# Expert layer's begin: last answers and logits ahead of the shared expert's products, its activations multiplied on GpSimd, running counts in three additions

## The reference, cut to what matters

```
normed = layernorm(x) * ln_gamma + ln_beta          # 1024 rows
logits = normed @ router_w.T                        # 8 experts
probs  = softmax(logits);  top_v, top_i = top_k(probs, 2);  gates = softmax(top_v)
for e in range(8): out += comb[:, e, None] * swiglu(normed, gate_up_w[e], down_w[e])
out += swiglu(normed, shared_gate_up_w, shared_down_w)     # silu(gate) * up @ down
x = x + out
```

## Time and profile before

| | before |
|---|---|
| median of 3 runs | 1829.05 us (1829.04 to 1835.1) |
| profiled execution, its own time | 1831.19 us |
| its span | 1829.30 us |
| granted TensorE clock, mean | 0.997 |
| TensorE busy | 1768.9 us, 97% |
| VectorE, ScalarE, GpSimd busy | 1347.6, 1018.4, 938.8 us |

### The profile page before, as it was taken

One profiled execution on the slowest core, in us unless ns is written; L12 is line 12 of the kernel. 1 busy time (PEld: TensorE's weight loads), 2 busy tenths in 40 slices (PEclk: granted clock), 3 DMA queues, 4 the chain that ended last, 5 costly groups with the idle time before them and its releaser, 6 DMA issues.

```text
span 1829.3 us, 44764 instructions
## 1 busy us (share of the span) xinstructions
PE 1768.9 (97%) x17870; PEld 1542.8 (84%) x17870; DVE 1347.6 (74%) x2790; ACT 1018.4 (56%) x2138; POOL 938.8 (51%) x1178
## 2 busy tenths in 40 slices
PE   7999999999999999999999999999999999999998
PEld 5888888888888778899999999999999986668887
DVE  6888888888888877667766767676777655767775
ACT  5677676767677745455444445444445434536664
POOL 3787877777777517445433334333433303524553
PEclk9999999999999999999999999999999999999999
DMA  6121111121110110044222222222223007051111
GB/s 166 38 74 39 38 39 38 53 59 38 38 38 3 60 51 1 26 120 117 64 64 64 64 64 64 64 64 64 77 76 87 15 1 304 1 187 32 33 32 16
DMA packets 50750, 113.11 MB, mean 62 GB/s; under 512 B 4928, under 2 KB 37264, under 8 KB 49008
## 3 DMA queue, kind: packets, MB, share of 16 engines
q1 hardware_dynamic: 46128, 105.13, 19.4%
q0 software_dynamic: 4416, 5.12, 1.6%
HBM read 105.78 MB, written 5.37 MB: 61 GB/s over the span
## 4 chain that ended last, share of the span: by engine, by line
PE 77%; DVE 13%; ACT 4%; issue 3%; DMA 2%; POOL 1%; SPq 0%; DVEq 0%; POOLq 0%; ACTq 0%
PE ps L104 8%; PE ps L166 7%; PE ps L1782 5%; PE ps L514 5%; PE ps L495 5%; PE ps L472 4%; DVE arenaR L1899 3%; PE ps L2769 3%; DVE arena L1905 3%; PE ps L1783 3%; PE ps L489 3%; PE ps L424 2%; PE ps L1706 2%; PE ps L2743 2%; PE ps L2744 2%
## 5 line engine op out<-in xcount | busy, mean ns | idle before, releaser
L617 DVE TENSOR_REDUCE arena<-ps 128x1 f32<-128x400 f32 (+1 forms) x512 | 257.7, 565 | 84.8 <-PE ps L472 84.4
L777 ACT ACTIVATE arena<-ps 128x384 f32<-128x384 f32 (+1 forms) x512 | 223.3, 524 | 95.0 <-PE ps L495 93.8
L1782 PE MATMUL ps<-arenaR 128*128 128x386 f32 x768 | 266.3, 392 | 1.4 <-DVE arenaR L1899 1.4
L878 POOL TENSOR_TENSOR arena<-arena 128x512 f32<-128x512 f32 (+1 forms) x152 | 197.2, 1298 | 77.6 <-ACT arena L777 69.3
L2009 ACT CAST arenaR<-ps 128x512 fp32r<-128x512 f32 (+1 forms) x256 | 123.0, 507 | 184.0 <-PE ps L166 175.0
L1783 PE MATMUL ps<-arenaR 128*128 128x194 f32 x768 | 194.8, 254 | 0.0
L166 PE MATMUL ps<-ident,wsb 128*128 128x128 f32 (+1 forms) x832 | 160.0, 273 | 5.0 <-DVE arenaR L1899 3.0
L2034 ACT ACTIVATE wsb<-ps,arena 128x1200 f32<-128x1200 f32 x64 | 80.9, 1264 | 132.0 <-DVE arena L1958 132.0
L1782 PEld LDWEIGHTS ps<-arenaR 128*128 128x128 f32 x768 | 145.5, 189 | 1.7 <-DVE arenaR L1899 1.6
L1783 PEld LDWEIGHTS ps<-arenaR 128*128 128x128 f32 x768 | 146.8, 191 | 0.0
L1899 DVE TENSOR_TENSOR arenaR<-ps,arenaR 128x512 fp32r<-128x512 f32 (+1 forms) x256 | 138.2, 581 | 4.0 <-ACT arenaR L2009 3.7
(11 more groups left out here) (387 smaller groups left out, 5098.2 us busy)
## 6 DMA issues: line engine op xcount, KB each, us to landing
wsb<-in_ctx SPq DMA_DIRECT2D x16, 1152.0 KB
wsb<-in_ctxT SPq DMA_DIRECT2D x16, 800.5 KB, 5.1
wsb<-in_ctxT SPq DMA_DIRECT2D x32, 400.2 KB, 7.6
gu<-in_m_gu SPq DMA_DIRECT2D x8, 1536.0 KB, 19.5
arena<-in_ctxT SPq DMA_DIRECT2D x15, 800.5 KB, 5.0
arena<-in_ctxT SPq DMA_DIRECT2D x30, 400.2 KB, 7.3
dn<-in_m_dn SPq DMA_DIRECT2D x8, 768.0 KB, 11.3
wsb<-in_f_w SPq DMA_DIRECT2D x2, 1024.0 KB, 5.8
```

The source lines that it names most:

```text
L617: e.tensor_reduce(mx4[n % 2][:, u, i:i + 1], ps[:, at("look", n, i, u), 0:400 + (i == 3)], AX.X, ALU.max).then_inc(c.maxed.at((n, i, u)), 1)
L777: e.activation(v[:, u, 0:128 * GN[s]], ps[:, at("st", n, s, u), 0:128 * GN[s]], ACT.Exp).then_inc(c.exp_a.at((x0, n, s, u)), 1)
L878: e.tensor_tensor(sums_p[0:k], sums_p[0:k], v[0:k, :, 128 * t:128 * t + 128], ALU.add).then_inc(added_p.at((n, s)), 1)
L1782: e.matmul(o, PTh[:, t, :], v[:, t, 0:386], start=(t == 0), stop=False)
```

## The change

On TensorE the last answers are turned ahead of any logits, and all logits come before the first shared product: tile 7 is turned behind the logits of tile 4, its halves into two banks (2 and 3), each with its own signal. VectorE adds the last answers before it norms tile 6. The second half of tile 7's `hT` is taken by ScalarE, behind the load of its Exp table, the first by VectorE as before. `shared_gu(0, 0)` is made whole behind the logits; ranks come between it and `shared_gu(0, 1)`; `shared_gu(1, 1)` stands behind the table, and `shared_down(1)` behind `turn_block(0)` (on VectorE behind `take_block(0)`).

The product Silu x up moves from VectorE to GpSimd. As GpSimd can't read PSUM, ScalarE copies up into `sT` ahead of the Silu, and GpSimd multiplies in place: the first two ahead of the gates' product, (1, 0) ahead of the first gather, (1, 1) between the second and the third.

The running counts, before a masked 128x512 product and a sum over it (and one addition for `cnt`), are made by copying the counts behind 64 zeros (which GpSimd writes) and three additions, each of the counts and the counts 1, 2 and 4 tiles back; `base` and `cnt` are views of the result.

```diff
@@ moe, pe: logits, and the order
-            w.wait_ge(*(c.hT_act((into, t)) if t < LT else c.hT_dve((into, t))))
+            w.wait_ge(*c.hT_act((into, t)))
+            if t == LT:
+                w.wait_ge(*c.hT_dve((into, t)))
...
         tail.turn_rows(e, w, LT - 2, 6, 256)
-        logits(0)
-        logits(1)
         tail.turn_answers(e, w, LT, 2, 0)
+        for t in range(3):
+            logits(t)
         w.wait_ge(*c.hT_act((into, LT - 2)))
         tail.turn_rows(e, w, LT - 1, 6, 0)
-        for t in range(2, 5):
+        for t in range(3, 5):
+            logits(t)
+        w.wait_ge(*c.x_new((tt, LT)))
+        w.wait_ge(*c.normed((into, LT)))
+        for k in range(2):
+            c.turn(e, ps[:, 2 + k, 256:384], c.h[:, LT, 128 * k:128 * k + 128]).then_inc(c.hT_turned.at((into, LT, k)), 1)
+        for t in range(5, NT):
             logits(t)
         ended(w)
-        shared_gu(0, 0, (0,))
-        w.wait_ge(*c.x_new((tt, LT)))
-        tail.turn_rows(e, w, LT, 2, 256)
-        for t in range(5, NT):
-            logits(t)
-        shared_gu(0, 0, (1,))
-        shared_gu(0, 1)
+        shared_gu(0, 0)
         w.wait_ge(*routing("chosen"))
         e.matmul(ps[:, 7, 0:64], tri, flat(M), start=True, stop=True)
         e.matmul(ps[:, 7, 64:128], ones, flat(M), start=True, stop=True).then_inc(routed.at("ranks"), 1)
+        shared_gu(0, 1)
         shared_gu(1, 0)
         shared_down(0, range(2))
-        shared_gu(1, 1)
         w.wait_ge(*routing("placed"))
         for k in range(2):
             table(k)
+        shared_gu(1, 1)
         shared_down(0, range(2, 4))
-        shared_down(1)
...
         turn_block(0)
+        shared_down(1)
@@ moe, dve
-        def shared_act(half, f):
-            w.wait_ge(*sh_silu((half, f)))
-            if half:
-                w.wait_ge(*h_out("h"))
-            e.tensor_tensor(sT[half][:, f, :], ps[:, sh_bank(half, f) + 1, :], sgs[f], ALU.mult).then_inc(sh_act.at((half, f)), 1)
...
-        norm_tile(c, e, w, into, LT - 1)
         tail.add_answers(e, w, LT, 2, 0)
         w.wait_ge(*c.x_new((tt, LT)))
         moments(c, e, w, into, LT)
+        norm_tile(c, e, w, into, LT - 1)
...
-        w.wait_ge(*c.hT_turned((into, LT)))
-        for k in range(2):
-            e.tensor_scalar(hT[:, k, 128 * LT:1024], ps[:, 2, 256 + 128 * k:384 + 128 * k], c.lng[:, k:k + 1], c.lnb[:, k:k + 1],
-                            ALU.mult, ALU.add).then_inc(c.hT_dve.at((into, LT) if k else None), 1)
+        w.wait_ge(*c.hT_turned((into, LT, 0)))
+        e.tensor_scalar(hT[:, 0, 128 * LT:1024], ps[:, 2, 256:384], c.lng[:, 0:1], c.lnb[:, 0:1],
+                        ALU.mult, ALU.add).then_inc(c.hT_dve.at((into, LT)), 1)
...
-        e.tensor_tensor(c4, ps[:, 7, 64:128].rearrange("p (u e) -> p e u", e=8).unsqueeze(1).broadcast_to([128, 8, 8, 8]),
-                        lt.unsqueeze(2).broadcast_to([128, 8, 8, 8]), ALU.mult).then_inc(c.dv.at(), 1)
+        w.wait_ge(*c.po("past the last"))
+        e.tensor_copy(Z[0][:, 8:16, :], T).then_inc(c.dv.at(), 1)
         w.wait_ge(*c.dv.now())
-        e.tensor_reduce(base, c4, AX.X, ALU.add).then_inc(c.dv.at(), 1)
-        w.wait_ge(*c.dv.now())
-        e.tensor_tensor(cnt, base[:, 7, :], T[:, 7, :], ALU.add).then_inc(c.dv.at(), 1)
-        w.wait_ge(*c.dv.now())
+        for i, back in enumerate((1, 2, 4)):
+            src, dst = Z[i % 2], Z[1 - i % 2]
+            e.tensor_tensor(dst[:, 8:16, :], src[:, 8:16, :], src[:, 8 - back:16 - back, :], ALU.add).then_inc(c.dv.at(), 1)
+            w.wait_ge(*c.dv.now())
...
-        for f in range(2):
-            shared_act(0, f)
...
-        for f in range(2):
-            shared_act(1, f)
...
         shared_down(0)
+        take_block(0)
         shared_down(1)
-        take_block(0)
@@ moe, act
+            if half:
+                w.wait_ge(*h_out("h"))
+            e.copy(sT[half][:, f, :], ps[:, sh_bank(half, f) + 1, :]).then_inc(sh_silu.at(), 1)
             e.activation(sgs[f], ps[:, sh_bank(half, f), :], ACT.Silu).then_inc(sh_silu.at((half, f)), 1)
...
         e.activation(c.sd[:, 1:2], c.ident[:, 0:1], ACT.Exp).then_inc(c.ac.at(), 1)
+        w.wait_ge(*c.hT_turned((into, LT, 1)))
+        e.activation(hT[:, 1, 128 * LT:1024], ps[:, 3, 256:384], ACT.Identity, bias=c.lnb[:, 1:2], scale=c.lng[:, 1:2]
+                     ).then_inc(c.hT_act.at((into, LT)), 1)
@@ moe, pool
+        def shared_act(half, f):
+            w.wait_ge(*sh_silu((half, f)))
+            e.tensor_tensor(sT[half][:, f, :], sT[half][:, f, :], sgs[f], ALU.mult).then_inc(sh_act.at((half, f)), 1)
...
+        for i in range(2):
+            e.memset(cmp_[:, 128 * i:128 * i + 64], 0.0).then_inc(c.po.at(), 1)
         e.memset(C_[:, :, NS:NS + 1], 0.0).then_inc(c.po.at("past the last"), 1)
+        for f in range(2):
+            shared_act(0, f)
         w.wait_ge(*routing("placed"))
...
-        for i in range(3):
-            gather(i)
+        shared_act(1, 0)
+        gather(0)
+        gather(1)
+        shared_act(1, 1)
+        gather(2)
```

More of the change, by code:

```diff
@@ L2626, in moe @@
     yS = [ar(128, 256) for _ in range(2)]
-    lg, pr, oh1, oh2, tmp, M, base, slot = [ar(128, NT, 8) for _ in range(8)]
-    cnt, nt, start, end = [ar(128, 8) for _ in range(4)]
+    lg, pr, oh1, oh2, tmp, M, slot = [ar(128, NT, 8) for _ in range(7)]
+    nt, start, end = [ar(128, 8) for _ in range(3)]
     pos, blk, row, g12 = [ar(128, 16) for _ in range(4)]
@@ L2910, in dve @@
         T = ps[:, 7, 64:128].rearrange("p (t e) -> p t e", e=8)
-        c4 = cmp_.rearrange("p (t e u) -> p t e u", e=8, u=8)
-        c3 = cmp_[:, 0:64].rearrange("p (a b) -> p a b", b=8)
+        Z = [cmp_[:, 128 * i:128 * i + 128].rearrange("p (t e) -> p t e", e=8) for i in range(2)]
+        base, cnt = Z[1][:, 7:15, :], Z[1][:, 15, :]
+        c3 = cmp_[:, 256:320].rearrange("p (a b) -> p a b", b=8)
         w.wait_ge(*prob("gate"))
@@ L2945, in dve @@
             w.wait_ge(*c.dv.now())
-        w.wait_ge(*c.po("past the last"))
         ce = cmp_[:, 0:16 * NS].rearrange("p (i s) -> p i s", s=NS)
```

## The result

The changed kernel is slower: ratio to the kernel before 1.0031, with a 95% interval of 1.0021 to 1.0042, which is 5.7 us (3.9 to 7.7). Its eleven runs took 1836.05 to 1844.96 us (median 1838.85), eleven runs of the kernel before, the three shown ahead of the prediction among them, 1829.04 to 1841.71 (median 1834.10). The forecast was 0.4 us faster, within 1826.5 to 1831.3. The profiled execution of the changed kernel took 1836.66 us, its span is 1834.8, 5.5 more than before.

What follows compares the result with a forecast made beforehand. TensorE, busy 97% of the span, bounds the kernel, so the change acts only by moving the start of `gate_up(0, 0)`. Terms on its path summed to -0.4 us: from the median 1829.05 to 1828.7, range 1826.5 to 1831.3.

Steps and rivals of the forecast that it cites:

- A rule against the change: VectorE's routing chain beside GpSimd's products: lengthening taken from the median row, 691 against 619, 0.1 us per us, hidden.
- The price at the worst: GpSimd's two products hold VectorE's chain fully, 2.6 us: rows ready at 1632.3, 1.1 behind TensorE; sum +0.7.
- The case: Rival, VectorE's routing chain held by GpSimd: 1.1 us later than forecast, time 1829.8; chance 0.05.
- the clock behind the table: TensorE behind the table's narrow products: no lower clock, as wide products stand ahead and behind; -1.2 to -1.6 us, 1.3 taken.
- the rival's price of +1.3: Rival, second slow stretch stays: lower clock behind the table falls on `shared_gu(1, 1)`, +1.3 us, time 1830.0; chance 0.25.
- The rivals: Second slow stretch stays (0.25), VectorE held by GpSimd (0.05), routing chain is what counts (0.08), clock returns early (0.14).
- the logits 1.2 us earlier: Last logits, made ahead of the first shared product: at 1616.9 instead of 1618.1, 1.2 us earlier, 2.3 at most.
- the ranks 1.1 earlier: Ranks' products on TensorE behind `shared_gu(0, 0)`: out at 1622.4 where VectorE took them at 1623.80; 1.3 us earlier.
- the gap ahead of the last tile's turn: TensorE waits ahead of the last logits, as the last tile is normed 0.45 us later, at 1613.8; its turn ends at 1614.4.
- the first stretch at 0.50: Lower clock after the last steps' small turns and logits: 3.0 us of it on `shared_gu(0, 0)`, costing 1.5 us.
- the wait of 0.59 for product (1, 1): TensorE ahead of `shared_down(1)`: new stall of 0.6 us for GpSimd's product (1, 1), ready at 1641.35.
- `take_block(0)`'s wait: TensorE's 1.35 us wait for VectorE ahead of `gate_up(0, 0)`: gone, as `take_block(0)` is done under `shared_down(1)`.

Runs made afterwards that it cites:

- a_pieces: The changed kernel with each GpSimd product made as four 128x128 instructions instead of one 128x512; ratio to the kernel before 1.0016, median 1837.40 us.
- a_filler: The changed kernel with 1.7 us of useless wide TensorE work in the idle ahead of the table; ratio to the kernel before 1.0000, median 1834.54 us.
- a_gu11_ahead: The changed kernel with `shared_gu(1, 1)` ahead of the table again, products still on GpSimd; ratio to the kernel before 1.0006, median 1834.45 us.
- b_counts: The kernel before with only the running counts made by three additions; ratio to the kernel before 0.9998, median 1832.82 us.
- b_counts_turn: The kernel before with the new running counts, and `turn_block(0)` and `take_block(0)` ahead of the last tile of `shared_down(1)`; ratio 0.9996, median 1832.17 us.
- c_gate_early: The kernel before with the first half of `shared_gu(0, 0)` directly behind the last answers' turn; ratio 0.9987, median 1831.20 us.
- b_pool_products: The kernel before with the four Silu products on GpSimd and the copies of up on ScalarE; ratio 1.0018, median 1836.84 us.

## Why the prediction was wrong

**The step that failed** is the one headed "A rule against the change": "at the median of 691 against 619 it is 0.1 us for each us and hidden. I take the median." Measured, three operations were held for 3.1 us, not 0.3. The price at the worst ("If GpSimd's two products (2.6 us) held VectorE's chain fully") was near, and even it was low, since the third product, (1, 0), held the chain too and was left out. The case got a chance of 0.05. The row's median was the wrong end, and was no price of a meeting at all. Of the 76 executions of L646 that the timeline of the kernel before lists singly, 35 have no GpSimd instruction beside them, and these take 0.68 to 0.69; of the 16 above 0.8 every one has a GpSimd instruction beside it. The longest is the case to be looked at:

```profile
42.37 2.69 POOL L878 TENSOR_TENSOR arena<-arena 128x512 f32<-128x512 f32 x2
...
43.80 1.80 DVE L646 TENSOR_TENSOR arena<-arena 128x512 f32<-128x512 f32 x1
```

It ends 0.54 behind GpSimd's pair (45.06), as if it had run only then. That maximum was what a meeting can cost. The reason given, "the chain's operations are 64 elements wide", turned out to be the wrong way round: the wait does not scale with the width of the waiting operation, it lasts to the end of the GpSimd instruction (1.33 for 64 elements; 0.52 when that instruction was a quarter as long, in a_pieces).

**The second failed term** is the clock behind the table, "-1.2 to -1.6, of which I take 1.3", and with it the rival's price of +1.3. The rivals were added up as if they excluded each other. They do not: the late chain made the idle of 2.06 us, and idle and table were followed by a stretch at 0.50 of 10.2 us instead of 3.4, over the table (+2.4) and over `shared_gu(1, 1)` (+2.4). a_filler shows the link: chain held as before, no long idle, clock up, and both terms gone. So +1.3 should have been about +5: the rival priced the lower clock on part of `shared_gu(1, 1)`, and it lay over nearly all of the table and of the product behind it.

**Right:** the logits 1.2 us earlier (read 7.9 us after the answers against 9.1), the ranks 1.1 earlier (forecast 1.3), the gap ahead of the last tile's turn, the first stretch at 0.50 that runs on into `shared_gu(0, 0)` (5.44 for its eight records; forecast 5.0), the wait of 0.59 for product (1, 1) (forecast 0.6), `take_block(0)`'s wait gone, `shared_gu(1, 1)` as the gather's cover, the rounds behind untouched. Without GpSimd's products the same order comes out at 0.9994 of the kernel before, -1.1 us (-2.8 to +0.6), where the sum said -0.4; the interval takes in the sum and no change alike. TensorE waited for none of the clearing writes, the first three copies on ScalarE or the table load, as said. The sum to `gate_up(0, 0)`: -0.4 as forecast, +2.1 of idle ahead of the table (3.1 held, of which TensorE's own work covered the rest), +2.4 on the table and +2.4 on the product behind it: +6.5, against 6.3 in the profiles (42.5 less 36.2).

**The range** had a fault of its own: it was set around 1829.05, a median of three runs, while runs of the kernel before went from 1828.74 to 1849.38 in what followed, around a median near 1834. The mean granted clock listed with each run goes along with that. (1 - clock) x span, averaged over the 116 runs of the kernel before that stood beside the experiments, is 9.6 us; over the changed kernel's eleven it is 14.4. The difference, 4.8, is most of the loss of 5.7. Part of the spread arises far from the change: the profiled execution of a_gu11_ahead (1842.87) has 13.7 us at 0.50 from 707 us on, where the kernel before has none. What decides in single executions whether the clock falls and how long it stays is not settled here. An idle is not needed for a fall: in b_counts TensorE did not wait ahead of the table, and 3.4 us at 0.50 followed all the same, while the same table in b_counts_turn was followed by none. The profiles of the changed kernel and a_filler show what the idle of 2.06 us went with, not a rule for it.

## What to carry to other kernels

A GpSimd operation beside a chain of small VectorE operations is priced by its own length for each meeting of two instructions with two SBUF inputs, not by the share of width, and every operation that can meet it counts; take the maximum of the rows where both ran, not their median. An idle on TensorE is priced with what runs behind it: here two microseconds of waiting ahead of narrow products went with five more at the lower clock. Useful wide products in such a wait are worth trying, even ahead of more urgent work (c_gate_early, 2.4 us). Rivals that can bring each other about are not alternatives, and need a case of their own.

## What the runs showed of the hardware

VectorE's operations with two SBUF inputs do not share time with a GpSimd `tensor_tensor` on SBUF. Whichever starts second waits for the other: 64 elements took 1.33 us instead of 0.23, and GpSimd's product 1.86 instead of 1.27 behind a 1024-element row. One-input reductions beside a product kept their 0.22 (L2924 and L2929 of b_pool_products, beside the 2.50 us of GpSimd). With a one-input GpSimd operation the roles turn (L2934 +0.45, GpSimd 1.49 to 2.48). The Trainium skill ("GPSIMD Engine Reference", Specifications) names the contention and the two-input condition; the traces agree, and give it the size of a whole instruction. And a kernel became faster by work on TensorE whose result nobody reads: 1.7 us of wide products ahead of the table won 5.7 us (about 1.9 to 9.5) against the changed kernel.
